# Scaled keys moved behind the value projections on ScalarE, with two token-major key buffers

## The reference

```
def step(S, inp):
    qt, kt, vt, gt, bt = inp
    S = S * jnp.exp(gt)[..., None, None]
    pred = jnp.einsum('bhk,bhkv->bhv', kt, S)
    u = (vt - pred) * bt[..., None]
    S = S + jnp.einsum('bhk,bhv->bhkv', kt, u)
    o = jnp.einsum('bhk,bhkv->bhv', qt, S)
    return (S, o)
_, oT = jax.lax.scan(step, S0, (qT, kT, vT, gT, bT))
...
var = jnp.mean(o * o, axis=-1, keepdims=True)
on = o * jax.lax.rsqrt(var + EPS) * norm_weight
on = on * jax.nn.silu(zg)
return on.reshape(Bb, Tt, VAL_DIM) @ W_out
```

## Time and profile before

| What | Value |
|---|---|
| median of 3 runs | 4840.66 us (4827.86 to 4842.49) |
| the profiled execution's own time | 4831.96 us |
| its span | 4830.2 us |
| PE busy | 4403.5 us (91%) |
| DVE busy | 3866.0 us (80%) |
| ACT busy | 2975.3 us (62%) |
| POOL busy | 1012.1 us (21%) |
| slots of layer 0 | start 741.3 us, last one 2414.1 us |
| slots of layer 1 | start 3107.9 us, last one 4796.8 us |

### The profile page before, as it was taken

How to read it: one execution, slowest core, us unless ns; L and a number is a source line. 1 busy time by engine, 2 the same in 40 slices (tenths; PEclk the granted TensorE clock), 3 DMA queues, 4 the chain that set the end, 5 groups by cost and what they waited for, 6 DMA issues and landing times. The chain is left out here.

```text
span 4830.2 us, 93590 instructions
## 1 busy us (share of the span) xinstructions
PE 4403.5 (91%) x32596; PEld 3615.9 (75%) x32596; DVE 3866.0 (80%) x8126; ACT 2975.3 (62%) x9834; POOL 1012.1 (21%) x1252
## 2 busy tenths in 40 slices
PE   5899939999999999999959998399999999999998
PEld 3578827888888888888845877388888888888887
DVE  6938988888888888888841599788888888888886
ACT  1146626777777777777711665366766667676665
POOL 0024411222212121212200344012121212121211
PEclk8999969999999999999979999699999999999999
DMA  1035642222222222223210566222222222222222
GB/s 56 30 91 174 189 137 70 82 75 83 78 83 75 80 83 77 82 78 82 63 31 11 154 182 194 77 76 83 76 74 81 78 81 81 75 85 74 76 76 64
DMA packets 580414, 422.57 MB, mean 87 GB/s; under 512 B 392808, under 2 KB 476312, under 8 KB 579502
## 3 DMA queue, kind: packets, MB, share of 16 engines
q1 hardware_dynamic: 563566, 408.20, 28.9%
q0 software_dynamic: 16384, 8.42, 1.1%
HBM read 296.24 MB, written 120.16 MB: 86 GB/s over the span
## 5 line engine op out<-in xcount | busy, mean ns | idle before, releaser
L1228 DVE SCALAR_TENSOR_TENSOR conv_l<-mix_l,taps_l,conv_l 128x512 f32<-128x512 f32 x1152 | 861.1, 757 | 156.0 <-ACT conv_l L1051 125.5
L854 PE MATMUL pj_l<-x_high,w_high_l 128*128 128x512 f32 x1280 | 572.7, 447 | 159.5 <-ACT w_high_l L1060 159.5
L1431 POOL TENSOR_TENSOR fac_l<-den_l,powers 128x4 f32<-128x4 f32 x256 | 258.9, 1012 | 1596.9 <-DVE den_l L1352 1595.3
L1196 ACT ACTIVATE Z_l<-gb_l 128x128 f32<-128x128 f32 x1024 | 266.6, 290 | 490.9 <-PE gb_l L1014 490.9
L854 PE MATMUL pj_l<-x_high,w_low_l 128*128 128x512 f32 x1280 | 519.0, 405 | 16.9 <-DVE W_l L1316 16.7
L854 PE MATMUL pj_l<-x_low,w_high_l 128*128 128x512 f32 x1280 | 512.8, 401 | 0.0
L637 POOL DMA_DIRECT2D own_dram<-key_kkS_l x512 | 298.2, 589 | 915.5 <-ACT key_kkS_l L509 905.3
L1023 PE MATMUL gb_l<-wo_l,gT_l 128*128 128x256 f32 x2048 | 480.0, 384 | 0.0
L1023 PEld LDWEIGHTS gb_l<-wo_l,gT_l 128*128 128x128 f32 x2048 | 372.6, 190 | 69.7 <-ACT Z_l L1196 25.6
L1362 DVE SCALAR_TENSOR_TENSOR x<-gb_l,fac_l,x 128x256 f32<-128x256 f32 x1024 | 412.9, 476 | 11.4 <-POOL fac_l L1431 0.2
L854 PEld LDWEIGHTS pj_l<-x_high,w_high_l 128*128 128x128 f32 x1280 | 242.5, 189 | 217.5 <-ACT w_high_l L1060 159.9
(11 more groups left out here) (204 smaller groups left out, 10773.9 us busy)
## 6 DMA issues: line engine op xcount, KB each, us to landing
rows_l<-rows_dram SPq DMA_DIRECT2D x128, 1024.0 KB, 5.6
k_dram<-kT_l SPq DMA_DIRECT2D x128, 256.0 KB, 2.3
kk_dram<-key_kkS_l SPq DMA_DIRECT2D x128, 256.0 KB, 2.3
kq_l<-k_dram SPq DMA_DIRECT2D x128, 256.0 KB, 3.3
kkS_l<-kk_dram SPq DMA_DIRECT2D x128, 256.0 KB, 5.8
w_raw_l<-in_wx SPq DMA_DIRECT2D x32, 640.0 KB
lane_k_l<-own_dram SPq DMA_DIRECT2D x32, 512.0 KB, 4.1
t_dram<-lane_t_l SPq DMA_DIRECT2D x14, 1024.0 KB, 4.9
```

The source lines that it names most:

```text
L854: ins = nc.tensor.matmul(pj_bank(c, t), wt[:, k, t, :], xt[:, k, :, at], start=(k == 0 and n == 0), stop=(k == KD - 1 and n == 2))
L1196: ins = nc.scalar.activation(Z[:, g, bank(b)], gb[:, 0, g, bank(b)], ACT.Square, accum_out=ss_o[:, g, b:b + 1])
L1228: ins = nc.vector.scalar_tensor_tensor(out, mix[:, t, :, i:i + P], wt(i), out, ALU.mult, ALU.add)
L1431: nc.gpsimd.tensor_tensor(fac[:, g, :], den[:, g, :], m.powers[:, 1, :], ALU.pow).then_inc(fac_ok[g], 1)
```

## The change

`ktok` gets a second buffer, chosen by the chunk's parity, and `square_keys` waits for keys one chunk further back. `scaled_keys` leaves the start of the slot. For c = 1 and 2 both groups are made in the same slot behind the silus of the values (L1073) and ahead of the last two weight roundings and of `y` (L1187). For c = 0 they are made in the last slot of the head in front, between the output copies (in layer 1: the copies of `y`) and the squares. Those of the first head's chunk 0 are made ahead of the first slot. No instruction is added or dropped.

```
-        ktok = sb("ktok", [P, WIDE])
+        ktok = sb("ktok", [P, 2, WIDE])
...
                     act.wait_ge(ktok_mm, q + 1)
                     if not first:
-                        act.wait_ge(ke_ok, 6 * h + 2 * c)
-                    nc.scalar.activation(ktok[:, :], kk[:, 0, :], ACT.Copy).then_inc(ktok_cp, 1)
+                        act.wait_ge(ke_ok, 6 * h + 2 * max(0, c - 1))
+                    nc.scalar.activation(ktok[:, q % 2, :], kk[:, 0, :], ACT.Copy).then_inc(ktok_cp, 1)
...
-                        ins = nc.scalar.activation(ke[:, g, bank(b)], ktok[:, bank(b)], ACT.Copy, scale=last)
+                        ins = nc.scalar.activation(ke[:, g, bank(b)], ktok[:, q % 2, bank(b)], ACT.Copy, scale=last)
...
                     nh, ncn = following(h, c)
-                    if c < CHUNKS - 1:
-                        scaled_keys(h, c, 0)
                     if not last:
                         copy_mix(nh, ncn, 0, False)
                     copy_z32(it)
-                    if c < CHUNKS - 1:
-                        scaled_keys(h, c, 1)
                     if not last:
...
                         for t in range(1, CONVS):
                             silu_conv(nh, ncn, t)
+                    if 0 < c < CHUNKS - 1:
+                        for g in range(GROUPS):
+                            scaled_keys(h, c, g)
                     if c == 2 and h < KHEADS - 1:
...
                             nc.scalar.activation(oT[:, g, :], gb[:, 1, g, :], ACT.Copy).then_inc(o_cp[g], 1)
+                    if c == CHUNKS - 1 and not last:
+                        for g in range(GROUPS):
+                            scaled_keys(nh, ncn, g)
                     for g in range(GROUPS):
...
                 scaled_values(0, 0)
+                for g in range(GROUPS):
+                    scaled_keys(0, 0, g)
                 steps(body)
```

## The result

The changed kernel takes 4770.29 us (median of 4 runs, 4767.27 to 4774.79) against 4839.26 us of the kernel before (4 runs, 4827.86 to 4842.49): a ratio of 0.9862, with a 95% interval of 0.9844 to 0.9881. It is about 69 us faster, and 13 us under the forecast of 4783 us. Its profiled execution took 4774.79 us, with a span of 4773.0 us.

What follows compares the result with a forecast made beforehand. Slot starts were held by ScalarE, busy with keys. Gains of 26.4 (c = 0), 23.7 (c = 1) and 10.5 us (c = 2), less 2.3 (first slots) and 0.8 (c = 3), make 57.5: 4840.66 to 4783 us, range 4768 to 4798.

Steps and rivals of the forecast that it cites:

- The start of c = 1: Slot of chunk 1, start: with keys gone `W_l` begins at 3.34 us instead of 4.08; gain 0.74 us.
- The middle of c = 1: Chunk 1 before `y`: 2.34 us of keys fit ScalarE's 3.01 us idle time, scans don't wait; no cost.
- The middle of c = 2: Chunk 2: roundings behind the keys end at 16.32 us, the scan starts at 16.73 instead of 17.03; gain 0.30 us.
- c = 3: End of chunk 3's slot: 2.34 us of keys go into 2.35 us idle in layer 0; cost 0.05 us.
- c = 0: Start of chunk 0's slot: taps come earlier without meeting GpSimd; gain 0.88 us in each of 30 slots.
- A layer's first slot: Both key groups stand ahead of L1118's copy, for which TensorE already waits; cost 1.17 us, twice.
- The whole 1.07 us in every slot: Rival: each of 96 slots gains the 1.07 us by which chunk 3's `W_l` is earlier; 4740 us; chance 0.12.
- taps held in full: Rival: tap pair ends 1.54 us behind `qd_l`, `W_l` 0.20 us later in chunks 1 and 2; 4796 us; chance 0.12.
- Keys dearer than their pitch: Rival: a key costs over 0.29 us; no change around 0.43 (chance 0.09), slower if dearer (0.05), 4899 us at 0.52.

Runs made afterwards that it cites:

- experiment 4: Changed kernel, but GpSimd makes `qd_l` for the next chunk in the slot before, not at the slot's start: 4758.06 us, ratio 0.9837.
- Experiments 1 and 2: Changed kernel with, in chunk 2, last two roundings ahead of keys: 4752.38 us; changed kernel with group 0's keys early in chunks 1 and 2: 4749.36 us.
- Experiment 6: Changed kernel, but the eight keys in a head's last slot are made twice, once into a spare tile: 4815.29 us, ratio 0.9960.
- experiment 5: Changed kernel, but chunk 0's eight keys stand in their own slot behind L1118's copy, none in a head's last slot: 4799.67 us, ratio 0.9925.

## Why the prediction was right, and where it was off

**The start of c = 1** came out to the hundredth: 0.74 forecast, 0.74 measured. `W_l` is at 3.32 us, and experiment 4 shows the mechanism: `qd_l` holds the taps, and without it another 0.14 us go. The Trainium skill (SBUF — State Buffer, "Who interferes with whom") says that such a pair contends and that the shared ports are an exclusive lock, so that the second comer blocks fully. The trace doesn't bear out that form of it, if the profile's ends are taken as they stand. In the changed kernel `qd_l` ends at 1091.31 and the pair of taps at 1092.64, 1.33 us later and not 1.53, the pair's undisturbed length. The first tap begins 0.34 us before `qd_l` ends and becomes only 0.14 us longer. Why it isn't 0.34 stays open: the ends of GpSimd's instructions are rough in this profile. That the two contend at all, as the page says, experiment 4 confirms.

**The middle of c = 1** cost nothing, with 0.70 us of idle time left before `y`, as forecast, and no scan that waits for keys.

**The middle of c = 2** was right in each step: the roundings at 16.32 us, VectorE idle for 0.58 us, the scan at 16.72, and 0.31 us gained for 0.30. The estimate that ScalarE would be 1.0 us earlier came out at 1.00; that is in part luck, since the rows bounded it only from below, at 0.74. Experiments 1 and 2 show it from the other side: with the wait gone, 0.68 us more.

**c = 3** was taken at a loss of 0.05 and has none. Experiment 6 shows how close that was: the room was exactly full, and the next 2.34 us of keys cost 2.20.

**c = 0** is the term that was mis-sized: 0.88 forecast, 1.13 measured, 30 x 0.25 = 7.5 us in all. The step that failed is the gain taken from the start of the slot alone, the idle 0.80 us and the 0.08 of overlap on VectorE. It took `W_l` for what sets this slot, as it does in c = 1. `W_l` did move as forecast, to 3.19 us, but experiment 5 moves it alone and nothing is left at the slot's end. The second wait was to be seen in the trace of before, 0.39 us of TensorE's weight load at L883 for ScalarE's L1079, and the prediction didn't read that far into the slot: the two waits have one cause, ScalarE's list, and the later one decides. Once it is gone TensorE has hardly a gap there.

**A layer's first slot** is the other: 1.17 forecast, 2.03 measured. That both groups now stand ahead of L1118's copy was right, and L923 does come 1.16 us later (5.28 us into the slot, from 4.12). Where the clock stayed up the slot lost 26.73 - 25.80 = 0.93 us; the other 27.82 - 26.73 = 1.09 us came with the lower clock, which the prediction had put at nothing. It is 2 us of the whole.

By slots the change is worth 64.7 us in the profiled executions; 57.5 was forecast. The difference is c = 0's 7.5 us, with c = 3 and the first slots making small and opposite changes. From 4840.66 us that gives 4776; the remaining 6 us lie within the spread of the runs (15 us for the kernel before, 8 for the changed one), and no slot shows them. The measured time lies only 2 us above the low end of the forecast's own range, 4768 us. That end was worked out unevenly: 13 us of bounds and 7 of scatter, added up as at the upper end, would have given 4763.

**The rivals.** The whole 1.07 us in every slot is out: c = 1 has 0.74 and c = 2 has 0.31. So are taps held in full, by the 1.33 us above. Keys dearer than their pitch are out as well: from the start of one key to that of the next in a row it is 292 ns at the median in the kernel before and in the changed one, in all places, and in experiment 6, where they were doubled, four came at 1.17 us. That rival would have made the kernel slower, and it is the duration that suggested it.

## What to carry to other kernels

Ask of each stage separately what it waits for last, even if all are passes of one loop: an earlier `W_l` was worth all of itself in c = 1 and, alone, nothing in c = 0, where a second wait for the same busy engine stood 5 us further on. Follow the waiting engine to the end of the stage before pricing its first wait. Price instructions that stand back to back by the distance of their starts, not by their duration. And when work is moved into an idle stretch, look at what stands right behind it in the queue: in c = 2 the keys ate up most of the gain because a short instruction that another engine needed stood behind them, and swapping the two gave 18 us.

## What the runs showed of the hardware

One kind of instruction, the scaling of a key, took 0.52 us at its median before and 0.41 after, and in both kernels four of them held ScalarE for 1.17 us. So the duration in the profile isn't the time that such an instruction takes up in the queue, and 768 of them with 0.1 us less each made no time by that. The Trainium skill (ScalarE: Activation LUTs, "What ACT_TABLE_LOAD costs") has a formula for it: 186 ns and 0.833 ns an element, 93 ns more for a scale that is read from memory, and an overlap of 93 ns back to back. For 128 elements that is an estimate of 386 ns alone and 293 ns in a row. The trace agrees with the second, 292 ns from start to start; of the durations only the shortest, 386 ns, is the first number, and the others go up to 535 ns.

A wait of 1.98 us of TensorE early in a layer was followed by 3.7 us at a granted clock of 0.57, a wait of 1.60 us at the same place by 1.00, and 0.29 us in the kernel before by 1.00 too. The lower clock cost 1.09 us, a little more than the wait itself did to the slot (0.93 us). Of twelve such slots the five with waits of 1.89 to 2.00 us lost this 1.09 us and the seven with waits of 1.31 to 1.60 us didn't. As the waits were longer just where the granted clock ahead of them was higher (0.76 to 0.78 against 0.63 to 0.70), these runs don't show which of the two decides.
